# A DLRM tower on one core: a twelfth pair of tiles is split, and VectorE's low parts of layer 1 read copies in PSUM

## The reference

```python
    e = jnp.stack([tbl_0[ids[:, 0]], ..., tbl_38[ids[:, 38]]], axis=1)     # 2048 x 39 x 16
        for idx, (W, b) in enumerate(params):                             # three layers of 128
            z = jnp.einsum('bhd,bkd,hks->bsd', x0, xk, W) + b[None, :, None]
            z = jax.nn.relu(z)
            if idx != n_layers - 1:
                half = z.shape[1] // 2
                xk = z[:, :half, :]
                direct.append(z[:, half:, :])
            else:
                direct.append(z)
        logit = jnp.sum(jnp.concatenate(direct, axis=1), axis=-1)
    h = jnp.concatenate([z, dense_ctx], axis=1)
    h = jnp.maximum(h @ W_top1 + b_top1, 0.0)
    h = jnp.maximum(h @ W_top2 + b_top2, 0.0)
    y = h @ W_top3
```

## Time and profile before

| what | value |
|---|---|
| median of 3 runs | 2544.88 us (2543.24 to 2546.89) |
| the profiled execution: its own time, its span | 2545.02 us, 2543.1 us |
| PE, PEld busy in the span | 2432.8 us (96%), 1423.5 us (56%) |
| DVE busy | 2268.7 us (89%) |
| ACT busy | 1175.5 us (46%) |
| POOL busy | 1557.9 us (61%) |
| granted TensorE clock, mean of the span | 0.995 |

### The profile page before, as it was taken

One profiled execution on the slowest core, in us unless ns is written; L12 is line 12 of the kernel. 1 busy time (PEld: TensorE's weight loads), 2 busy tenths in 40 slices (PEclk: granted clock), 3 DMA queues, 4 the chain that ended last, 5 costly groups with the idle time before them and its releaser, 6 DMA issues.

```text
span 2543.1 us, 25999 instructions
## 1 busy us (share of the span) xinstructions
PE 2432.8 (96%) x7712; PEld 1423.5 (56%) x7712; DVE 2268.7 (89%) x1356; ACT 1175.5 (46%) x1414; POOL 1557.9 (61%) x1029
## 2 busy tenths in 40 slices
PE   0599999999999999999999999999999999999999
PEld 0265555556555555555555565555556555555553
DVE  0599999999999999999999999999999999999960
ACT  0244444445454444545444444444444444445442
POOL 6476667667666766766676666667666766743240
PEclk9899999999999999999999999999999999999999
DMA  2986777777677777867777776787777677766610
GB/s 69 246 211 180 199 207 202 180 217 214 176 198 205 207 178 215 209 182 197 209 206 177 217 206 190 190 211 210 178 207 205 200 184 213 207 182 194 195 30 0
DMA packets 262712, 477.02 MB, mean 188 GB/s; under 512 B 19500, under 2 KB 37788, under 8 KB 262614
## 3 DMA queue, kind: packets, MB, share of 16 engines
q1 hardware_dynamic: 141766, 271.07, 38.9%
q10 hardware_dynamic: 100480, 200.29, 28.5%
q0 software_dynamic: 20448, 5.45, 1.4%
HBM read 468.99 MB, written 7.74 MB: 187 GB/s over the span
## 4 chain that ended last, share of the span: by engine, by line
PE 73%; POOL 10%; DVE 6%; issue 4%; DMA 4%; ACT 2%; SPq 0%; POOLq 0%; DVEq 0%; ACTq 0%
PE z L693 37%; PE z L716 33%; POOL emb L352 5%; DVE prod L418 4%; POOL pair_lo L211 4%; DMA emb<-in_tbl,idx 3%; PE xk L775 1%; PE z L775 1%; DMA x_pairs<-x_transposed 1%; ACT pair_hi L532 1%; POOL half_parts L207 1%; DVE pair_lo L211 1%; PE turned L674 1%; DVE logit L448 1%; ACT xk L542 0%
## 5 line engine op out<-in xcount | busy, mean ns | idle before, releaser
L418 DVE TENSOR_TENSOR prod<-x_pairs,xk 128x2048 f32<-128x2048 f32 x640 | 1436.4, 2284 | 75.2 <-PE z L716 46.9
L693 PE MATMUL z<-prod,w_plain 128*128 128x512 f32 (+2 forms) x2944 | 1383.1, 594 | 40.5 <-DVE prod L418 40.5
L532 ACT CAST pair_hi<-prod 128x1024 fp32r<-128x1024 f32 x703 | 735.4, 1046 | 1085.2 <-PE z L716 793.6
L211 POOL TENSOR_TENSOR pair_lo<-prod,pair_hi 128x1024 fp32r<-128x1024 f32 x320 | 764.1, 2388 | 638.3 <-ACT pair_hi L532 621.7
L693 PEld LDWEIGHTS z<-prod,w_plain 128*128 128x128 f32 (+2 forms) x2944 | 555.4, 189 | 474.1 <-issue 394.9
L352 POOL DMA_INDIRECT emb<-in_tbl,idx x624 | 701.3, 1124 | 184.0 <-issue 173.7
L716 PE MATMUL z<-pair_hi,w_lo 128*128 128x512 f32 (+1 forms) x1408 | 786.6, 559 | 2.3 <-DVE pair_lo L211 1.7
L716 PE MATMUL z<-pair_hi,w_hi 128*128 128x512 f32 (+1 forms) x1408 | 555.7, 395 | 0.0
L716 PE MATMUL z<-pair_lo,w_hi 128*128 128x512 f32 (+1 forms) x1408 | 555.1, 394 | 0.0
L211 DVE TENSOR_TENSOR pair_lo<-prod,pair_hi 128x1024 fp32r<-128x1024 f32 (+1 forms) x384 | 468.5, 1220 | 48.7 <-ACT pair_hi L532 48.7
L716 PEld LDWEIGHTS z<-pair_hi,w_lo 128*128 128x128 f32 (+1 forms) x1408 | 265.2, 188 | 297.2 <-POOL pair_lo L211 135.8
(11 more groups left out here) (50 smaller groups left out, 566.5 us busy)
## 6 DMA issues: line engine op xcount, KB each, us to landing
x_pairs<-x_transposed SPq DMA_DIRECT2D x64, 2432.0 KB, 16.9
x_pairs<-x_transposed ACTq DMA_DIRECT2D x64, 2432.0 KB, 19.3
x_diag<-x_transposed SPq DMA_DIRECT2D x128, 546.0 KB
x_diag<-x_transposed ACTq DMA_DIRECT2D x64, 546.0 KB
x_pairs<-x_transposed SPq DMA_DIRECT2D x64, 256.0 KB, 20.4
emb<-in_tbl,idx POOLq DMA_INDIRECT x624, 6.3
x_diag<-x_transposed SPq DMA_DIRECT2D x128, 78.0 KB
x_transposed<-stage SPq DMA_DIRECT2D x32, 156.0 KB
```

Source lines behind the costliest of these rows:

```text
L211: engine.tensor_tensor(pair_lo[0:rows, pair % PAIR_RING], held[0:rows, at:at + 2, :], pair_hi[0:rows, pair % PAIR_RING].bitcast(F32), ALU. ...
L418: nc.vector.tensor_tensor(prod[0:rows, pos % RING, 0:n, :], a, xk.unsqueeze(1).broadcast_to([rows, n, N]), ALU.mult).then_inc(prod_ready, 1)
L532: nc.scalar.copy(pair_hi[0:rows, pair % PAIR_RING], held[:, at:at + 2, :]).then_inc(hi_ready, 1)
L693: ins = nc.tensor.matmul(z[n][:], w, held[0:rows, i, :], start=(k == 0 and i == plain[0]), stop=(k == last_slot and not here and i == plai ...
```

## The change

- Layer 0's second pair is split too (12 pairs in a chunk).
- Layer 1: the low of the pair in slot 2 goes to GpSimd. For the other four pairs and the half tile, ScalarE writes the hi part a second time, to a PSUM tensor (`hi_copy`, or `direct01` for the half tile), and VectorE's low reads that copy. There is one `hi_copy`, so the second copy waits for the low before it (`lo_ready[V]`).
- Layer 0's two lows stay on VectorE and read the hi part in SBUF.
- `hi_parts` and `lo_parts` hold six tiles (three pairs) in place of two pairs.
- `direct01` moves to PSUM, `xk0` shares the tensor of `xk2`, and the transposes' results share `hi_copy`. So TensorE transposes behind layer 0 in place of ahead of it, and `fill_stage` stands behind layer 2's `direct_0` on ScalarE.
- TensorE takes layer 0's second slot first, then the first slot with its two split pairs, and frees both slots at the end.
- GpSimd gathers between layer 1's low and layer 2's lows.
- The sums of a group are kept in windows of 128 columns and stored to DRAM by SyncE, two DMAs of 64 KB in a group, and loaded once for the top (TOP_DMAS 10 in place of 6).
- VectorE's lows lag their product by one slot everywhere.

```diff
-SPLITS = {0: [(0, 0, 2)],
-          1: [(0, 0, 2), (1, 0, 2), (2, 0, 2), (2, 3, 1), (3, 0, 2), (4, 0, 2)],
-          2: [(0, 0, 2), (1, 0, 2), (2, 0, 2), (2, 3, 1), (3, 0, 2), (4, 0, 2)]}
-EARLY = {1: 4, 2: 4}
+SPLITS = {0: [(0, 0, 2, V), (0, 2, 2, V)],
+          1: [(0, 0, 2, V), (1, 0, 2, V), (2, 0, 2, G), (2, 3, 1, V), (3, 0, 2, V), (4, 0, 2, V)],
+          2: [(0, 0, 2, G), (1, 0, 2, G), (2, 0, 2, G), (2, 3, 1, G), (3, 0, 2, G), (4, 0, 2, G)]}
+EARLY = {1: 5, 2: 4}
...
+                hi = (hi_copy[0:rows, 0:m, :] if copy else
+                      hi_parts[0:rows, place:place + m, :].bitcast(F32))
+                engine.tensor_tensor(lo_parts[0:rows, place:place + m, :], held[0:rows, at:at + m, :],
+                                     hi, ALU.subtract).then_inc(done, 1)
...
+                    done = lows_of(1, chunk, 0, split, pos)
+                    if c == 2 and len(fields_at[c]):
+                        start_group(bt + 2, False)
+                    gather(fields_at[c])
...
+                    lows_of(2, chunk, done, split, pos)
...
+                    if n and who == V:
...
+                                act.wait_ge(lo_ready[V],
+                                            len(SPLITS[0]) + chunk * LOWS_C[V] + last + 1)
+                            nc.scalar.copy(hi_copy[:, 0:m, :].bitcast(F32R), held[:, at:at + m, :]
+                                           ).then_inc(hi_copied, 1)
...
-                    if c == 1 and not last:
-                        fill_stage(bt + 1)
...
                         direct_0()
-                        pair = round_splits(SPLITS[2][EARLY[2]:], P, slot, pos, pair, held_by)
+                        if c == 1 and not last:
+                            fill_stage(bt + 1)
+
+                            act.wait_ge(stage_ready, 2 * (bt + 2))
+                        round_splits(2, slice(EARLY[2], None), slot, pos, used_by, chunk)
...
+            def layer0(slot, pos, lows):
+
+                pe.wait_ge(prod_ready, slot + SL0)
+                held = prod[:, (pos + SL0 - 1) % RING]
+                t = L0_FIRST[SL0 - 1]
+                for i in range(T0 - t):
+                    plain_part(0, t, i, held, i == 0, False)
...
+                for i, (s, place) in enumerate(zip(SPLITS[0], PLACES[0])):
+                    ins = split_part(0, 0, s, place, lows, False, i == len(SPLITS[0]) - 1)
+                    lows[s[3]] = lows[s[3]] + 1
+                ins.then_inc(slot_free, SL0)
```

More of the change, by code:

```diff
@@ L78 @@
 NB = 512
-assert CB < NB < B and len(SPLITS[0]) == 1
+assert CB < NB < B and all(k == 0 for k, _, _, _ in SPLITS[0])
 def top_order():
@@ L439, in subtract @@
-            def subtract(item, split, pair):
-                n, pos, at, m = item
-                dve.wait_ge(hi_ready, split + 1)
-                low_part(nc.vector, n, pos, at, m, pair)
-                return split + 1, pair + (m == 2)
-            def sum01(chunk):
-                dve.wait_ge(direct01_ready, 2 * chunk + 2)
-                nc.vector.tensor_reduce(logit01[:, bass.ds(chunk * CB, CB)],
+            def subtract(late, split):
+                for n, pos, copy, place, k, at, m, who in late:
+                    if who == V:
+                        if copy is None:
+                            dve.wait_ge(hi_ready, split + 1)
+                        else:
+                            dve.wait_ge(hi_copied, copy + 1)
+                        low_part(nc.vector, n, pos + k, at, m, place, copy is not None, lo_ready[V])
+                    split += 1
+                return split
@@ new lines, in splits_of, with products @@
+            def splits_of(n, pos, slot, chunk):
+                copies, here = lows(1, V) if n == 2 else 0, []
+                for s, place in zip(SPLITS[n], PLACES[n]):
+                    copy = chunk * COPIES_C + copies if n else None
+                    copies += s[3] == V
+                    if s[0] == slot:
+                        here.append((n, pos, copy, place, *s))
+                return here
+            def products(n, copies, xk, slot, pos, late, split, chunk):
+                first_tile, rows, tiles = (FIRST_TILE, P, TX) if n else (L0_FIRST, R0, T0)
+                for k, first in enumerate(first_tile):
+                    product(slot + k, pos + k, copies[0:rows, first:min(first + QUAD, tiles), :],
+                            xk[0:rows])
+                    split = subtract(late, split)
+                    late = splits_of(n, pos, k, chunk)
+                return late, split
@@ L456, in sum2 @@
                                         z[2][:].rearrange("p (d b) -> p b d", b=CB),
                                         AXIS.X, ALU.add).then_inc(summed2, 1)
-            def layer(n, copies, xk, slot, pos):
-                return [(n, k, copies, xk, slot + k, pos + k) for k in range(SLX if n else SL0)]
-            products(layer(0, x0_diag, xk0, 0, 0), 0, 0, 0)
+            dve.wait_ge(xk0_ready, 1)
+            late, split = products(0, x0_diag, xk0, 0, 0, [], 0, 0)
+            subtract(late, split)
@@ L525, in round_splits @@
+            def round_splits(n, some, slot, pos, used_by, chunk):
+                rows = P if n else R0
+                for i, ((k, at, m, who), place) in list(enumerate(zip(SPLITS[n], PLACES[n])))[some]:
                     act.wait_ge(prod_ready, slot + k + 1)
                     held = prod[0:rows, (pos + k) % RING]
-                    if n == 1:
+                    if m == 1:
                         nc.scalar.copy(half_parts[:], held[:, at, :]).then_inc(hi_ready, 1)
                     else:
-                        act.wait_ge(slot_free, RING + held_by[-PAIR_RING] + 1)
-                        nc.scalar.copy(pair_hi[0:rows, pair % PAIR_RING], held[:, at:at + 2, :]
+                        act.wait_ge(slot_free, RING + used_by[place + m - 1] + 1)
+                        nc.scalar.copy(hi_parts[0:rows, place:place + m, :], held[:, at:at + m, :]
@@ L613, in group @@
                         load_second_half(bt + 1, 0)
-                    pair = round_splits(SPLITS[1][:EARLY[1]], P, slot, pos, pair, held_by)
+                    round_splits(1, slice(0, EARLY[1]), slot, pos, used_by, chunk)
                     direct_2(chunk, slot)
@@ L689, in layer @@
                     pe.wait_ge(prod_ready, slot + k + 1)
                     for i in plain:
-                        rows = P if n else R0_LAST if t + i == T0 - 1 else R0
-                        w = whole[0:rows, PLAIN_TILES[n].index(t + i), :]
-                        ins = nc.tensor.matmul(z[n][:], w, held[0:rows, i, :],
-                                               start=(k == 0 and i == plain[0]),
-                                               stop=(k == last_slot and not here and i == plain[-1]))
@@ L720, in layer @@
-                    ins.then_inc(slot_free, 1)
-                return pair
+                        ins = plain_part(n, t, i, held, k == 0 and i == plain[0],
+                                         k == last_slot and not here and i == plain[-1])
+                    for i, (s, place) in enumerate(here):
+                        ins = split_part(n, t, s, place, lows, False,
+                                         k == last_slot and i == len(here) - 1)
+                        lows[s[3]] = lows[s[3]] + 1
```

297 lines of the change are left out of this document (167 added, 130 removed).

## The result

The changed kernel takes 2580.73 us (median of 4 runs, 2577.94 to 2581.72), the kernel before 2544.27 on the same chip: ratio 1.014, 95% interval 1.0122 to 1.0158. It is slower by 36 us, where the prediction of 2522 us was 23 less than before. The profiled execution's span is 2576.2 us, 33.1 longer.

The account below looks back on a forecast made before the run. TensorE was taken as the bound, with VectorE close behind. 63 chunks at -0.38 us give -23.9, plus 0.6 for start and end: -23, from 2545 to 2522 us. Own range 2514 to 2530; with rivals 2501 to 2544.

Parts of the forecast that it names:

- So they can run at 5 to 6 ... a wait of 0 to 1: Transposes can run 5 to 6 us behind layer 1's end; TensorE, through layer 0 at 5.4, waits 0 to 1.
- Or up to 1 later if gathers are held: Ninth gather starts about 1 us ahead of layer 1's end, or up to 1 us later if gathers are held.
- The second rival: Layer 0's two lows hold gathers 1.2 us each; transposes wait up to 2 more: 22 us, 2544; either half, chance 0.17.
- Its other half: Late `fill_stage` delays `x0_diag`; at 12 us beside ScalarE's transfer, VectorE is 2.2 late less 0.7 slack: 22 us.
- Layer 0's second pair: Splitting it saves 0.31 us of TensorE's work a chunk, but beside a fixed chain: costed at nothing in ordinary chunks.
- that of `direct01` in PSUM: Layer 2: `sum01` takes 687 ns in place of 1059, so slot 2's product, hi copy and low come 0.37 us sooner.
- The waits at slots 2 and 3: Layer 2: slot 2's wait of 0.19 us is covered, and all but some 0.05 of about 0.2 behind it.
- the predicted 0.38 a chunk: Gain from layer 2's waits: 0.34 us a chunk, up to 0.44; 0.38 taken.
- I had 0.7: VectorE idles about 0.7 us for xk2, its slack in a chunk.
- the third rival: VectorE becomes the bound: four pair lows each wait 0.77 us for second copies, +2.0 a chunk, 2671 us; chance 0.08.
- the start is 0.6 us later: Start and end: first xk0 copy precedes a DMA issue, so the last transfers come some 0.6 us later: +0.6.

Follow-up runs that it names:

- the kernel with nine gathers: Changed kernel with gathers in parts of 9, 11, 11 and 8, copy-out earlier, GpSimd's own low waited for first at layer 2's slot 0: 2511.46 us.
- the runs with gathers on time: Changed kernel with six or eight gathers in the transposes' chunk in place of nine: 2671.59 us with six, 2670.77 with eight.
- the kernel before with the late copy-out: Kernel before the change, with only ScalarE's copy-out of the transposes moved behind layer 2's `direct_0`: 2743.55 us.
- the one with the copy-out moved alone: Changed kernel, gathers as they are, with only the copy-out moved behind the hi copy of layer 2's slot 1: 2573.22 us.
- the kernel with six gathers and the early copy-out: Changed kernel with six gathers in the transposes' chunk and the copy-out behind the hi copy of layer 2's slot 1: 2572.88 us.
- the wait turned for all lows: Changed kernel with GpSimd waiting for its own last low first and the hi copy second, for all lows: 2580.54 us.

## Why the prediction was wrong

**The step that failed** is "So they can run at 5 to 6 ... a wait of 0 to 1". The transposes run 8.05 us behind layer 1's end, and TensorE is through layer 0 at 5.4, as I had it: a wait of 2.67. Of the 3.05 us above my 5.0, 0.33 is the first gather (at -10.67, I took -11), 1.87 is gathers held by VectorE, nearly all of it the one beside layer 0's lows, and 0.85 is the landing (6.85 on the mean of the loop, where I took 6.0 from a single row; before, the mean is 6.3). "Or up to 1 later if gathers are held" was too small: the row of 1.78 was beside one low of a pair, and here there are two in a row.

**What no case had** is the clock. The chunk without it would be 36.41 + 0.87 for the transposes + 2.68 of wait - 0.62 that slot 0 no longer waits = 39.34; it is 40.94, and the 1.6 left agree with 3.41 us at half the clock. Two stops of the same length in other runs that cost no clock give the same price (last section). So the late gathers cost 4.3 us a group, 64 in all, of which the wait is 40 and the clock 24. In the kernel with nine gathers the sum without both is 36.32 + 0.87 - 0.52 = 36.67, as measured: there the transposes cost 0.35 us a group.

**The second rival** had the place (gathers held by layer 0's lows) and not the size: it capped the added wait at 2 us and the cost at 22. Its other half, `x0_diag` landing late behind the late `fill_stage`, did not cost in the changed kernel, but the runs with gathers on time and the kernel before with the late copy-out show it to be real and seven to nine times as dear as my 1.5 us a group (46.67 against 36.67, 49.37 against 36.28): the load took 21 us from its issue to the copy, where I allowed 12 against 8.4 before. Two readings in that sum were off besides: before, `fill_stage` starts 2.7 us behind layer 1's end (1195.20) and not 5, and the copy to xk0 comes 27.8 behind it (1220.22) and not 26.8.

**What held.** Layer 0's second pair costs and earns nothing in an ordinary chunk: 36.42 without it, 36.41 with it, and slot 0's wait is 0.31 or 0.62. The gain is that of `direct01` in PSUM: 0.24 of 0.27 goes when it goes back, which makes `sum01` 1055 ns again and takes the half tile's second copy to SBUF too. The waits at slots 2 and 3 are gone. Of the predicted 0.38 a chunk, 0.27 came, and 0.09 of the difference is one more semaphore wait of GpSimd ahead of layer 2's first low, worked off after the hi copy's; turned round it gave 0.09 back. VectorE idles 0.97 us for xk2 (I had 0.7), its lows from PSUM take 1213 ns, and giving it the GpSimd low back costs 1.0 us in an ordinary chunk: the third rival's bound is near, and giving that low to GpSimd kept the change off it. Whether the start is 0.6 us later can't be read: the first two intervals of the changed kernel and of the one with the copy-out moved alone, which start alike, differ by 4.1 us (78.1 and 74.0).

**What stays open:** which of VectorE's products and ScalarE's order holds layer 2's slots 2 and 3 once slot 0 is free; by what rule two DMA queues share the engines; and why the same stop lowers the clock in one group and not in another.

## What to carry to other kernels

When a step moves behind another, list everything that has to be there for it and date each from the same event, with the mean and the worst of its landings, not one row. A late input can hide a late output: after mending one wait, read the next stage's loads before believing the gain. And a stop of TensorE of 2 to 3 us can cost more than half as much again in clock (1.6 us behind stops of 2.0 and 2.7 here), so a stop that looks cheap is priced with it.

## What the runs showed of the hardware

- The same stop costs the clock in some groups and not in others. In the kernel with six gathers and the early copy-out TensorE stops for 2.04 us until 501.59 and until 653.54 (rows above); behind the first stop the clock falls and behind the second it does not:

```profile
501.50:504.90 3.40, 3.31 (x8) 2.30 (x9) 2.67 (x2) 3.31 (x6) 3.24 (x3) 0.59 0.75 185
653.00:656.40 3.40, 2.86 (x11) 1.87 (x11) 3.40 (x3) 3.15 (x5) 3.24 (x3) 1.00 0.75 193
```

  The interval with this stop is 39.7 us in the eight groups with a stretch at 0.5 and 38.1 in the six without: 1.6 us for one stretch of 3.41 us, as in the changed kernel. The longer stop at the transposes was spared twice. In the changed kernel with the early copy-out alone the first stop is 2.8 us and its interval 39.56, where a later stop of 2.8 has 41.2 and a stretch at 0.5; the windows around the first show a clock of 1.00. With the wait turned for all lows, the last stop is 2.9 us and its interval 39.61, where one of 2.9 with the stretch has 41.1.

```profile
157.10:160.30 3.20, 0.53 (x4) 0.10 (x2) 3.20 (x3) 1.04 (x1) 2.96 (x2) 1.00 0.27 41
160.30:163.70 3.40, 3.40 (x16) 2.31 (x17) 2.90 (x2) 2.68 (x5) 2.19 (x2) 1.00 0.02 5
```

- VectorE's subtract of two SBUF tensors holds a gather of GpSimd: 0.94 us alone, 1.65 beside one, 2.83 beside two in a row. The held gather ends 0.8 us behind the last subtract (757.91 behind 757.08, and 610.15 behind 609.32 with one low). The same subtract with its second input in PSUM (751.95 to 753.16) ran beside gathers of 0.94 us. The Trainium skill, page "SBUF — State Buffer", section "Who interferes with whom", has that rule for GpSimd instructions that read SBUF, but infers that descriptor generation is spared by such a subtract; these gathers were not.
- While a load on ScalarE's queue ran, SyncE's queue moved no packet for 5.1 to 6.1 us, in each of 15 groups (table above).
